# GpSimd waits for the landing of every eighth gather of expert output rows

## The reference

```python
# first: 32 experts, 4 per token, gated
logits = flat @ router_w.T + router_bias
topk_scores, topk_idx = top_k(softmax(logits), 4)        # weights made to sum to 1
h = silu(einsum('nd,ehd->neh', flat, gate_w)) * einsum('nd,ehd->neh', flat, up_w)
expert_out = einsum('neh,edh->ned', h, down_w)
out = (take(expert_out, topk_idx) * topk_scores).sum(axis=1) + shared_expert(flat)
# second: 8 experts, 2 per token, hidden size 512, one silu, softmax over the two logits
```

## Time and profile before

| What | Value |
|---|---|
| Median of 3 timed runs | 1239.35 us (1238.33 to 1243.01) |
| Profiled execution, its own time | 1241.5 us |
| Its span | 1239.7 us |
| Busy: TensorE, VectorE, ScalarE, GpSimd | 72%, 63%, 51%, 41% |
| Gathers at L1123, layer 0 | x64, 65.7 us busy |
| Gathers at L1123, layer 1 | x64, 65.7 us busy |
| Granted TensorE clock | 0.843 |

### The profile page before, as it was taken

One profiled execution on the slowest core, in us unless ns is written; L12 is line 12 of the kernel. 1 busy time (PEld: TensorE's weight loads), 2 busy tenths in 40 slices (PEclk: granted clock), 3 DMA queues, 4 the chain that ended last, 5 costly groups with the idle time before them and its releaser, 6 DMA issues. The chain is left out here.

```text
span 1239.7 us, 19813 instructions
## 1 busy us (share of the span) xinstructions
PE 897.0 (72%) x5652; PEld 691.5 (56%) x5652; DVE 783.5 (63%) x2423; ACT 630.2 (51%) x1304; POOL 513.5 (41%) x634
## 2 busy tenths in 40 slices
PE   3796666664439999929974466677668999999910
PEld 2633555553328889929863134344457977777710
DVE  5489589998765657404777699999867411016436
ACT  4355677774833234414322566776665545555500
POOL 0003555554146666644773775000005662036055
PEclk9998777776559999969987778888777999999965
DMA  7950000000501146436543111000031132223032
GB/s 208 289 160 1 1 0 0 0 0 20 222 28 44 45 128 191 142 121 176 159 125 100 47 47 31 1 0 1 1 130 53 57 107 82 61 75 96 27 94 60
DMA packets 133844, 97.00 MB, mean 78 GB/s; under 512 B 11648, under 2 KB 125696, under 8 KB 132736
## 3 DMA queue, kind: packets, MB, share of 16 engines
q1 hardware_dynamic: 121472, 70.79, 19.1%
q0 software_dynamic: 12288, 25.19, 6.9%
HBM read 45.61 MB, written 50.33 MB: 77 GB/s over the span
## 5 line engine op out<-in xcount | busy, mean ns | idle before, releaser
L1110 POOL DMA_INDIRECT e_xs<-h_tok,rows_of x128 | 128.8, 1007 | 101.7 <-DVEq L1571 35.4
L739 ACT ACTIVATE mask<-ps_q,k_neg 128x256 bf16<-128x256 f32 x256 | 101.0, 489 | 37.3 <-PE ps_q L853 37.3
L1123 POOL DMA_INDIRECT e_got<-e_ys,e_rows_of x64 | 65.7, 1027 | 127.1 <-DMA e_ys<-e_y_rows 108.2
L1259 PE MATMUL e_ps_gu<-e_w_all,e_x_turned 128*128 x384 | 96.9, 398 | 12.8 <-DVE e_hidden L1729 12.7
L1738 DVE COPY e_y_rows<-e_ps_y 128x512 f32<-128x512 f32 x20 | 13.8, 692 | 137.9 <-PE e_ps_y L1307 137.9
L853 PE MATMUL ps_q<-q_parts,pick 128*128 (+1 forms) x256 | 59.4, 368 | 48.9 <-DVE mask L651 42.1
L1442 ACT ACTIVATE e_hidden<-e_ps_up 128x512 f32<-128x512 f32 x80 | 47.8, 597 | 84.2 <-PE e_ps_up L1289 84.2
L2226 POOL DMA_INDIRECT c_got<-e_ys,rows_of x64 | 71.2, 1112 | 36.2 <-issue 19.2
L1110 POOL DMA_INDIRECT e_xs<-h_tok,e_rows_of x64 | 65.5, 1024 | 49.4 <-DVEq L1571 17.1
L1259 PEld LDWEIGHTS e_ps_gu<-e_w_all,e_x_turned 128*128 128x128 f32 x384 | 72.5, 199 | 23.0 <-issue 14.4
L1437 ACT ACTIVATE e_hidden<-e_ps_gu 128x512 f32<-128x512 f32 x48 | 28.7, 598 | 110.4 <-PE e_ps_gu L1259 110.4
(11 more groups left out here) (403 smaller groups left out, 2499.3 us busy)
## 6 DMA issues: line engine op xcount, KB each, us to landing
e_x_rows<-e_xs SPq DMA_DIRECT2D x68, 256.0 KB, 2.8
e_ys<-e_y_rows SPq DMA_DIRECT2D x68, 256.0 KB, 2.3
e_xs<-zeros SPq DMA_DIRECT2D x2, 6144.0 KB, 34.2
e_w_all<-in_w SPq DMA_DIRECT2D x4, 1536.0 KB, 13.5
e_xs<-zeros SPq DMA_DIRECT2D x2, 2560.0 KB, 27.4
e_w_all<-in_w SPq DMA_DIRECT2D x4, 1024.0 KB, 10.9
x_tok<-in_x SPq DMA_DIRECT2D x4, 512.0 KB, 6.2
e_xs<-h_tok,rows_of POOLq DMA_INDIRECT x128, 2.2
```

The costliest lines, as they stand in the source:

```text
L739: last = nc.scalar.activation(mask[u][QS // 2 + j][keys][:, h * T:(h + 1) * T], psq[1][:, h * T:(h + 1) * T], ACT.Sign, bias=k_neg[u][:, k ...
L1110: nc.gpsimd.indirect_dma_start(out=xs[part], out_offset=bass.IndirectOffsetOnAxis(ap=rows_of[:, t * K + k:t * K + k + 1], axis=0), in_=til ...
L1123: nc.gpsimd.indirect_dma_start(out=got[t % GB][:, k * P:(k + 1) * P], out_offset=None, in_=ys[part], in_offset=bass.IndirectOffsetOnAxis(a ...
L1259: last = nc.tensor.matmul(ps_gu[n % 2][:, t * 2 * P:(t + 1) * 2 * P], x_turned[n % 2][:, t * P:(t + 1) * P], at(w_all, col, 2 * P), start= ...
```

## The change

Behind the last gather of a tile, if the number of gathers so far is a multiple of 8, GpSimd waits for the gathers of that tile. In layer 0 that is every second tile, in layer 1 every fourth.

```diff
                                 out=got[t % GB][:, k * P:(k + 1) * P], out_offset=None, in_=ys[part],
                                 in_offset=bass.IndirectOffsetOnAxis(ap=rows_of[:, t * K + k:t * K + k + 1], axis=0),
                                 bounds_check=ROWS - 1).then_inc(gathered[t % GB], 16)
+                        if (t + 1) * K % 8 == 0:
+                            pool.wait_ge(gathered[t % GB], 16 * K * (t // GB + 1))
```

## The result

The changed kernel took 1264.65 us (median of 4 runs, 1263.26 to 1265.94), the kernel before 1239.84 beside it: ratio 1.0195, 95% interval 1.0179 to 1.021. It is slower by 24.8 us (the medians' difference; the interval is 22 to 26), where the prediction had 24.5. On other chips, on which the kernel before needs some 1350 us, the same change made it 1.1% faster; the experiments come to that. Chips on which the kernel before takes some 1240 us are called the first kind here, those on which it takes some 1350 the second.

The account below looks back on a forecast made before the run. The prediction took GpSimd's pace of issuing gathers to bound the first expert layer and gather landings the second layer's tail; 18.2 + 6.3 = 24.5 us on 1239.35 made 1263.9, given as 1264, range 1256 to 1271.

Parts of the forecast that it names:

- The price of a wait: In GpSimd's gathers, one wait costs landing + 0.82 - 1.32: 2.6 us taken in the first layer, 2.1 in the second.
- ten waits: The waits expected to delay the kernel: seven in the first layer, three in the second layer's second half, 24.5 us.
- the dearer end for the first layer: First-layer price set at 2.6 us, above the median's 2.4, because some gathers there land slowly.
- the 14 of the prediction: About 14 waits of 2.4 to 2.9 us, expected in GpSimd's idle time before L1123 in the profile after.
- First layer, all seven on the path: Seven waits with gathers behind them all delay tile 15's landing: 7 x 2.6 = 18.2 us.
- The eighth wait: First layer, behind tile 15: covered by GpSimd's 17.00 us idle before the next phase's first gather; at most 3 us otherwise.
- Second layer, first half at nothing: Waits behind tiles 3, 7, 11 and 15 are hidden and cost nothing; 1.4 us late at 3.3 a wait.
- The 2.2 us that I counted as left: Second layer, first half: slack between tile 14's delayed landing at 1147.3 and VectorE's combine of it at 1149.53.
- Second layer, second half: Three of the waits behind tiles 19, 23, 27 and 31 stand on the chain: 3 x 2.1 = 6.3 us.
- Rival A, TensorE's clock: First layer: TensorE stays at 1.2 GHz and becomes the bound, 7.0 us a step, 1271.3 us timed; chance 0.10.
- B: The first layer hides its waits and only the tail's 6.3 us show, 1245.7 us; chance 0.04.
- C: Not slower, because gathers run faster behind an emptied queue; 0.26 us saved for each would cancel the cost; chance 0.03.

Follow-up runs that it names:

- b_before: The kernel before, unchanged, run again for a second trace, on the first kind of chip: 1241.63 us beside 1239.58.
- f1_layer0: Against the kernel before, the waits in the first expert layer only, on the first kind of chip: 1258.29 us, ratio 1.014.
- f2_layer1: Against the kernel before, the waits in the second expert layer only, on the first kind of chip: 1246.59 us, ratio 1.0053.
- f4_each_tile: Against the kernel before, a wait behind every tile's four gathers, first expert layer only, on the first kind of chip: 1277.17 us, ratio 1.0292.
- e5_change: The changed kernel itself, timed beside the kernel before on the second kind of chip: 1338.69 us, ratio 0.9885.
- e3_old: Against the kernel before, waits at the change's places, but for gathers of two tiles earlier, on the second kind of chip: 1350.92 us, ratio 1.0049.
- e2_layer1: Against the kernel before, the waits in the second expert layer only, on the second kind of chip: 1342.73 us, ratio 0.9981.
- e1_layer0: Against the kernel before, the waits in the first expert layer only, on the second kind of chip: 1334.49 us, ratio 0.9894.
- e4_each_tile: Against the kernel before, a wait behind every tile's four gathers, first expert layer only, on the second kind of chip: 1352.23 us, ratio 1.0064.
- e6_spread: Against the kernel before, no waits for landings but a spare-buffer fill behind each first-layer gather, on the first kind of chip: 1254.43 us, ratio 1.0104.

## Why the prediction was right

*The price of a wait* came from the scatters and the landings: 2.6 us in the first layer, 2.1 in the second. Measured: the gathers of the first layer span 669.93 - 568.70 = 101.23 us instead of 83.85 (83.41 in `b_before`), which makes 2.5 for each of seven; those of the second layer's second half (47.40 - 41.42) / 3 = 2.0. By the Trainium skill ("DMA: Bandwidth & Descriptors", section "Anatomy of one DMA — SWDGE (gpsimd) path") ten waits would have been an estimate of 16.5 us; the 24.8 measured decide against it. To take the dearer end for the first layer was right in direction (3.03, 3.50 and 3.71 us of idle time occur beside 2.39) and some 0.1 too much in size. The longest, 3.71 less the 0.30 of every gather, is 3.4 and so just above the 3.3 that was given as the most that a wait can cost. The traces show 13 such waits, seven and six, 12 of them put down to landings, and not the 14 of the prediction: of the second layer's seven with gathers behind them one lies in the 37.32 us.

*First layer, all seven on the path.* 18.2 forecast, 17.4 by `f1_layer0`, 17.9 between the two marks of the traces. VectorE combines tile 15 at 673.24, 104.5 us behind the first gather instead of 86.6, and still waits for a landing there (2.97 us). The eighth wait was covered: GpSimd's idle time before 672.87 went from 17.00 to 17.55 only.

*Second layer, first half at nothing.* Right: 86.91 us from first gather to first gather in both traces. The 2.2 us that I counted as left sufficed, although one of the waits was of 3.13.

*Second layer, second half.* 6.3 forecast, 6.0 in the trace, 6.6 by `f2_layer1`.

*The sum.* 24.5 against 24.8 timed. The profile's spans differ by less, 1261.3 - 1239.7 = 21.6, since the first gather comes 2.3 us earlier in the trace after, ahead of everything that was changed; between two profiles one has to compare stretches, not spans. The stretches give 17.9 + 6.0 = 23.9, 0.8 us fewer between the layers, and 0.8 more behind the last gather; two traces of the kernel before differ by 2.1 between the layers.

*Rival A, TensorE's clock.* The windows of the trace after (busy of PE, PEld, DVE, ACT, POOL, then the granted clock):

```profile
618.00:624.00 6.00, 5.95 (x28) 5.36 (x29) 3.96 (x16) 1.79 (x3) 3.01 (x4) 0.72 0.44 120
624.00:630.00 6.00, 2.97 (x22) 2.60 (x20) 2.43 (x9) 1.58 (x3) 4.78 (x5) 0.95 0.54 142
630.00:636.00 6.00, 5.25 (x16) 4.43 (x17) 3.49 (x13) 1.18 (x2) 1.99 (x3) 0.50 0.39 112
636.00:642.00 6.00, 4.70 (x34) 4.26 (x32) 3.73 (x12) 2.19 (x5) 4.48 (x6) 0.98 0.41 116
```

In these windows the clock fell to 0.72 and to 0.50 (1.2 GHz all through) and was back at 0.95 and 0.98 in the next. The slow steps were made up for in time that TensorE would have idled: with 15 waits in `f4_each_tile` the cost of one did not grow (2.4). Rivals B and C fall too, B by `f1_layer0`, C by the durations (1010 ns at the median with and without waits). All of this holds for the first kind of chip. On the second kind the prediction's main step fails, that VectorE waits for the gathers: without the waits it waits for none of them in the first layer there. The prediction had no rival for that. That the result was measured on the kind of chip from which the trace came was luck; the mechanism on that kind was not.

## What to carry to other kernels

A wait for landing inside a series of indirect gathers costs the landing plus the restart, less the pace of one gather, 2.0 to 2.5 us on average here, and costs it in full wherever the consumer already waits for the series; one finds out by the waits of the consumer at that place, not by shares of the whole span. The same arithmetic read backwards finds time: the waits for landings that a kernel already has are priced by their own rows, and those without cover can go (1240 to 1217 us here). If the engine that waits can change with the chip, the sign of such a change can too, so it is timed on more than one (whether it is the chip that changes, or its condition, is open here).

## What the runs showed that was not expected

On the second kind of chip, instructions of VectorE, like those of TensorE above, often start 0.7 or 1.4 us apart while gathers follow each other closely. From `e5_change`, the combines of the RWKV block:

```profile
754.57 0.61 DVE L2008 SCALAR_TENSOR_TENSOR y_tok<-c_got,weight,y_tok 128x128 f32<-128x128 f32 x2 [1.05 <-DVE y_tok L2008]
755.99 0.35 DVE L2008 SCALAR_TENSOR_TENSOR y_tok<-c_got,weight,y_tok 128x128 f32<-128x128 f32 x1 [0.81 <-DVE y_tok L2008]
757.39 0.35 DVE L2008 SCALAR_TENSOR_TENSOR y_tok<-c_got,weight,y_tok 128x128 f32<-128x128 f32 x1 [1.05 <-DVE y_tok L2008]
758.82 0.35 DVE L2008 SCALAR_TENSOR_TENSOR y_tok<-c_got,weight,y_tok 128x128 f32<-128x128 f32 x1 [1.08 <-DVE y_tok L2008]
760.22 0.35 DVE L2008 SCALAR_TENSOR_TENSOR y_tok<-c_got,weight,y_tok 128x128 f32<-128x128 f32 x1 [1.05 <-DVE y_tok L2008]
```

The same instructions in the trace of the same kernel on the first kind:

```profile
736.26 4.29 DVE L2008 SCALAR_TENSOR_TENSOR y_tok<-c_got,weight,y_tok 128x128 f32<-128x128 f32 x16
```

16 of them in 4.29 us there, 0.27 each; here one takes 0.35 and then 1.05 us pass without work. The stretch ends just behind the last gather of that loop, issued at 787.11: until 791.04 GpSimd's own semaphore instructions come 0.7 or 1.4 us apart too, then mostly 0.07. In `e3_old`, whose first gather of the series is at 579.81, such a stretch begins near 587 and ends when the series has paused, because GpSimd waits there for a late combine:

```profile
606.95 1.01 POOL L1123 DMA_INDIRECT e_got<-e_ys,rows_of  x1 [6.32 <-DVE y_tok L1686]
```

Two traces of the changed kernel, of the first kind and of the second: first scatter at 348.5 and 351.6, first gather 568.7 and 583.0, the second layer's first scatter 953.4 and 997.7, its gathers 1114.7 and 1181.5 and, in the second half, 1201.7 and 1279.5. The lag grows from 3 to 78 us. Taken on VectorE, it grows beyond the first 3 us only while scatters or gathers are issued: 13 us at 749, 44.5 at 791, just behind the RWKV block's last gather, and 44.3 still at 998, where the next scatters begin. A chip slower all over (theory U) would not do that. Durations of the gathers (1.01 us) and the prices of the waits are the same on both kinds, and so is the granted clock nearly (0.829 against 0.836).

From that, pauses in the series give the other engines time back on the second kind. The traces bear it out. For the stretch from the first gather to the next phase's first, the table adds up the idle time that the profile puts down to no instruction of the core ("issue" or "remote" in the place of the releaser), one trace each:

| Run, second kind | Pauses for landings | VectorE | TensorE | Stretch | Stretch, first kind |
|---|---|---|---|---|---|
| `e3_old` | none | 42.0 us | 22.0 us | 128.5 us | not run |
| `e2_layer1` | none | 25.4 | 24.9 | 132.8 | 101.8 |
| `e5_change` | 7 | 16.1 | 10.8 | 117.0 | 119.8 |
| `e1_layer0` | 7 | 13.4 | 5.7 | 118.9 | 118.8 |
| `e4_each_tile` | 15 | 3.6 | 0 | 138.5 | 139.3 |

In the six traces of the first kind that were gone through, this idle time is 0 on both engines. With 7 pauses the stretch is about as long as on the first kind, and with 15 nothing is left to give back, which is why `e4_each_tile` loses again. What remains open: why instructions start so late there, whether it is the chip or its condition at that hour, whether it takes an emptied queue or only fewer transfers (`e6_spread` was to tell and met the first kind), and whether the removed scatter waits, worth 24.5 us on the first kind, would lose there. No run settles these.
